# Cross-attention of a decoder kernel: the row maximum is subtracted by GpSimd in SBUF, the scores are turned by transposes, and the first layer is spread over all heads

## What is computed

```python
out_mem = _mlp(*upd, k_flat).reshape(x_in.shape)        # silu(x @ w1.T + b1) @ w2.T + b2
g1 = jax.nn.sigmoid(out_swa @ lin1.T)
g2 = jax.nn.sigmoid(out_mem @ lin2.T)
out_merged = g1 * out_swa + g2 * out_mem
x = _layernorm(x + out_merged[:, NUM_PM:, :], axis=-1)
# _L0_xattn_ref
q, k, v = proj(query, wq, bq), proj(key, wk, bk), proj(value, wv, bv)
scores = jnp.einsum('bhqd,bhkd->bhqk', q, k) / np.sqrt(KEY_SIZE)
scores = jnp.where(mask[:, None, :, :], scores, -1000000000.0)
attn = jax.nn.softmax(scores, axis=-1)
x = jnp.einsum('bhqk,bhkd->bhqd', attn, v)
```

## Time and profile before

| | us |
|---|---|
| median of three runs | 1099.61 (1094.72 to 1112.12) |
| the profiled execution | 1108.69 |
| its span, first to last instruction | 1106.6 |
| PE busy | 789.4 (71%) |
| DVE busy | 529.8 (48%) |
| ACT busy | 394.6 (36%) |
| POOL busy | 132.5 (12%) |
| chain that ended last | PE 55%, DVE 20%, issue 9%, ACT 7%, DMA 6% |

### The profile page before, as it was taken

One profiled execution on the slowest core, in us unless ns is written; L12 is line 12 of the kernel. 1 busy time (PEld: TensorE's weight loads), 2 busy tenths in 40 slices (PEclk: granted clock), 3 DMA queues, 4 the chain that ended last, 5 costly groups with the idle time before them and its releaser, 6 DMA issues.

```text
span 1106.6 us, 14903 instructions
## 1 busy us (share of the span) xinstructions
PE 789.4 (71%) x4778; PEld 519.8 (47%) x4778; DVE 529.8 (48%) x1947; ACT 394.6 (36%) x924; POOL 132.5 (12%) x143
## 2 busy tenths in 40 slices
PE   5888687968444986968958829992665675684674
PEld 4445353534121653644735617782453462462462
DVE  4244253433233936936838321113456456446556
ACT  3514344351112542633623513330343243243343
POOL 9100000000101013013021040003200300300000
PEclk8797998999566997987977959996886786886887
DMA  7400000000116044072050011311100100100000
GB/s 217 142 10 10 1 19 0 19 0 0 53 37 87 1 60 84 3 79 62 15 64 13 1 45 35 102 37 44 39 10 0 48 9 0 47 9 0 10 0 10
DMA packets 49235, 39.36 MB, mean 36 GB/s; under 512 B 11234, under 2 KB 42658, under 8 KB 49188
## 3 DMA queue, kind: packets, MB, share of 16 engines
q1 hardware_dynamic: 47140, 34.62, 14.9%
q0 software_dynamic: 2048, 4.20, 1.3%
HBM read 27.20 MB, written 11.60 MB: 35 GB/s over the span
## 4 chain that ended last, share of the span: by engine, by line
PE 55%; DVE 20%; issue 9%; ACT 7%; DMA 6%; SPq 2%; POOL 1%; DVEq 1%; ACTq 0%; POOLq 0%
PE bank L1292 4%; DMA q_stack<-parts_dram 4%; PE bank L1213 4%; PE bank L1202 4%; DVE R L2064 2%; PE bank L1096 2%; PE bank L954 2%; PE bank L1016 2%; PE bank L1099 2%; PE bank L1109 2%; PE bank L1098 2%; PE bank L886 2%; PE bank L1068 2%; PE bank L1023 2%; PE bank L977 2%
## 5 line engine op out<-in xcount | busy, mean ns | idle before, releaser
L1813 DVE CUSTOM_DVE_ANT_0 bank<-bank,add_q 128x256 f32<-128x256 f32 x256 | 100.5, 457 | 51.2 <-PE bank L1068 39.3
L1507 ACT ACTIVATE pT<-bank 128x512 f32<-128x512 f32 x128 | 76.1, 597 | 76.7 <-PE bank L1099 74.4
L1068 PE MATMUL bank<-k_stack,q_stack 96*128 96x256 bf16 x256 | 52.5, 306 | 45.8 <-DMA q_stack<-parts_dram 39.4
L1232 PE MATMUL bank<-ident,X 128*128 128x128 f32 x48 | 14.2, 419 | 85.3 <-DVE X L1921 85.3
L1096 PE MATMUL bank<-q_stack,k_stack 96*128 96x256 bf16 x256 | 70.4, 275 | 1.2 <-DVE mx L1813 1.2
L1098 PE MATMUL bank<-add_k,ident_b 128*128 128x256 bf16 x256 | 70.6, 276 | 0.0
L1099 PE MATMUL bank<-neg_max,head_sel 96*128 96x256 bf16 x256 | 70.5, 276 | 0.0
L1292 PE MATMUL bank<-XT,kpad 128*128 128x256 f32 (+1 forms) x256 | 62.3, 373 | 0.0
L1068 PEld LDWEIGHTS bank<-k_stack,q_stack 96*128 96x128 bf16 x256 | 25.8, 107 | 71.1 <-DMA q_stack<-parts_dram 33.6
L2021 DVE TENSOR_TENSOR cT<-bank,decay 128x384 f32<-128x384 f32 x64 | 35.7, 558 | 47.1 <-ACT decay L1585 46.8
L1532 ACT ACTIVATE he<-bank 128x324 f32<-128x324 f32 x64 | 28.2, 440 | 69.5 <-PE bank L1202 64.0
(11 more groups left out here) (402 smaller groups left out, 1807.1 us busy)
## 6 DMA issues: line engine op xcount, KB each, us to landing
k_stack<-parts_dram SPq DMA_DIRECT2D x48, 64.0 KB
q_stack<-parts_dram SPq DMA_DIRECT2D x24, 128.0 KB, 11.8
expert_in<-no_rows SPq DMA_DIRECT2D x8, 324.0 KB, 4.0
rows<-expert_in SPq DMA_DIRECT2D x8, 324.0 KB
expert_out<-rows_y SPq DMA_DIRECT2D x8, 324.0 KB
moe_w<-in_L_ffn_w_dram SPq DMA_DIRECT2D x1, 2048.0 KB
parts_dram<-k_parts SPq DMA_DIRECT2D x4, 384.0 KB, 2.5
parts_dram<-q_parts SPq DMA_DIRECT2D x12, 128.0 KB, 1.7
```

The lines of the kernel that those rows point to most:

```text
L1068: last = pe.matmul(q_bank(n)[:, c * S:(c + 1) * S], q_stack[:, h // 2, b * S + c * P:b * S + (c + 1) * P], k_stack[:, h // 2, h % 2, b * S ...
L1507: act.activation(pT[:, g % 2, j], k_bank(n)[:].rearrange("p (c q) -> p c q", c=QC), ACT.Exp).then_inc(exp_ready.sem, 1)
L1813: last = dve.tensor_tensor_reduce(sc, sc, add_q[:, b * QC + c, :], 1.0, 2.0 * NEG, ALU.add, ALU.max, mx[:, c, h:h + 1])
```

## The change

The second set of scores, the transposes of the maxima, `negated`, `mask_k` and `add_k` go. A head is now: PE makes its scores with the query on the partitions (`scores`, three heads ahead); DVE adds the mask, writes the result to SBUF (`shifted`, four slots) and takes the row maximum; GpSimd subtracts the maximum in place, by two instructions of 128x256; PE turns the four 128x128 blocks by f32 transposes (`scores_T`) into one of two PSUM banks; ACT takes the exponential. The MLP's Silu becomes Tanh and a biased copy (`z_of`) on ACT and a multiplication on DVE, with the factor 0.5 taken later. `keys` and `head` now stand between the heads by `pe_at`, `act_at` and `dve_at`. `stack` is split: `stack_k(0)` stands ahead of `save_q(0)`, and in the loop both are issued when the last scores are made. The outputs are turned and divided in halves.

```diff
-        AHEAD = 14
...
+        LEAD = 3
+        SLIDE = 4
+        s_shifted = signal("s_shifted", XU)
...
-            return bank[4 + n % 4] if n < 12 else (bank[4], bank[5], bank[2])[n % 3]
+            return bank[4 + n % 3]
...
-        def k_bank(n):
-            return bank[6 + n % 2] if n < 20 else bank[4 + n % 4]
+        def sT_bank(n):
+            return (bank[7], bank[3])[n % 2]
...
+        pe_at = {3: 0, 5: 1, 7: 2, 9: 3, 11: 4, 13: 5, 15: 6, 18: 7, 23: 8, 25: 9}
+        act_at = {3: 0, 5: 1, 7: 2, 9: 3, 11: 4, 15: 6, 21: 7, 23: 8}
+        dve_at = {7: 0, 9: 1, 11: 2, 13: 3, 15: 4, 17: 5, 19: 6, 22: 7, 25: 8, 28: 9}
+        o_at = {21: 0, 23: 1}
...
             save_k(0)
+            stack_k(0)
             save_q(0)
-            stack(0)
+            stack_q(0)
...
-                    sp.wait_ge(*sT_ready.at(i))
-                    stack(i + 1)
+                    sp.wait_ge(*s_ready.at(i))
+                    stack_k(i + 1)
+                    stack_q(i + 1)
...
-                pool.tensor_scalar(add_q[:], mask_q[:], -1.0, -NEG, ALU.add, ALU.mult)
-                pool.tensor_scalar(add_k[:], mask_k[:], -1.0, -NEG, ALU.add, ALU.mult).then_inc(masks_ready.sem, 1)
+                pool.tensor_scalar(add_q[:], mask_q[:], -1.0, -NEG, ALU.add, ALU.mult).then_inc(masks_ready.sem, 1)
...
             def mix(i, following):
+                for n in range(XU):
+                    wait_apart(pool, passed, *s_read.at(i, n + 1))
+                    for c in range(QC):
+                        last = pool.tensor_scalar(shifted[:, n % SLIDE, c, :], shifted[:, n % SLIDE, c, :], mx[:, n % SLIDE, c:c + 1], None, ALU.subtract)
+                    last.then_inc(s_shifted.sem, 1)
+                    if following and n == 4:
+                        split_k(i + 1)
                 if following:
-                    split_k(i + 1)
-                    wait_apart(pool, passed, *sT_ready.at(i))
                     masks(i + 1)
...
-                def scores_q(n):
+                pe.wait_ge(*slots_ready.before(i))
...
-                        pe.wait_ge(*s_read.at(i, n - 3 if n < 14 else n - 2))
+                    if n >= 3:
+                        pe.wait_ge(*s_read.at(i, n - 2))
...
+                def scores_T(n):
+
+                    pe.wait_ge(*s_shifted.at(i, n + 1))
+                    if n >= 2:
+                        pe.wait_ge(*exp_ready.at(i, n - 1))
...
-                        pe.matmul(dst, k_stack[:, h // 2, h % 2, b * S + c * P:b * S + (c + 1) * P],
-                                  q_stack[:, h // 2, b * S:(b + 1) * S], start=True, stop=False)
-                        pe.matmul(dst, ident_b[:], add_k[:, b * QC + c, :], start=False, stop=False)
-                        last = pe.matmul(dst, head_sel[:, h % 8, :], neg_max[:, (n // 8) % 2, :], start=False, stop=True)
+                        for k in range(QC):
+                            last = pe.transpose(sT_bank(n)[:, k * S + c * P:k * S + (c + 1) * P], shifted[:, n % SLIDE, c, k * P:(k + 1) * P], ident[:])
                     last.then_inc(sT_ready.sem, 1)
 
...
-                        values((g - 1) // G, (g - 1) % G)
-                outputs_T(1)
+                for n in range(LEAD):
+                    scores(n)
+                for n in range(XU):
+                    if n + LEAD < XU:
+                        scores(n + LEAD)
+                    scores_T(n)
+                    if n >= 5 and n % 4 == 1:
+                        values((n // 4 - 1) // G, (n // 4 - 1) % G)
+                    if n in o_at:
+                        outputs_T(0, o_at[n])
+                    if following and n == 1:
+                        keys(i + 1)
+                    if following and n in pe_at:
+                        head(i + 1, pe_at[n])
+                values(NB - 1, G - 1)
+                for c in range(QC):
+                    outputs_T(1, c)
                 if following:
-                    pe.wait_ge(*exp_ready.at(i))
+                    pe.wait_ge(*s_read.at(i))
+                    pe.wait_ge(*pv_ready.at(i))
                     values_of(i + 1)
...
                     act.wait_ge(*zT_b.at(i, n + 1))
-                    act.activation(hT[:, n, 0:T], bank[1][:], ACT.Silu, bias=b1_new[:, n:n + 1]).then_inc(hT_b.sem, 1)
+                    if n == 0 and not is_first(i):
+                        act.wait_ge(*x_plus.before(i))
+                    if n >= 2:
+                        act.wait_ge(*hT_b.at(i, n - 1))
+                    act.activation(hT[:, n, 0:T], bank[1][:], ACT.Tanh, bias=b1_half[:, n:n + 1], scale=0.5)
+                    act.activation(z_of[n % 2], bank[1][:], ACT.Identity, bias=b1_new[:, n:n + 1]).then_inc(z_act.sem, 1)
...
-                if following:
-                    keys(i + 1)
-                    for n in range(5):
-                        head(i + 1, n)
...
+                    if following and n == 1:
+                        keys(i + 1)
+                    if following and n in act_at:
+                        head(i + 1, act_at[n])
...
+                if n < FC:
+                    dve.wait_ge(*z_act.at(i, n + 1))
+                    dve.scalar_tensor_tensor(hT[:, n, 0:T], hT[:, n, 0:T], 1.0, z_of[n % 2], ALU.add, ALU.mult).then_inc(hT_b.sem, 1)
...
-                def negated(m):
...
                     wait_apart(dve, passed, *s_ready.at(i, n + 1))
+                    if n >= SLIDE:
+                        wait_apart(dve, passed, *sT_ready.at(i, n - SLIDE + 1))
                     for c in range(QC):
-                        sc = q_bank(n)[:, c * S:(c + 1) * S]
-                        last = dve.tensor_tensor_reduce(sc, sc, add_q[:, b * QC + c, :], 1.0,
-                                                        2.0 * NEG, ALU.add, ALU.max, mx[:, c, h:h + 1])
+                        last = dve.tensor_tensor_reduce(shifted[:, n % SLIDE, c, :], q_bank(n)[:, c * S:(c + 1) * S], add_q[:, b * QC + c, :], 1.0,
+                                                        2.0 * NEG, ALU.add, ALU.max, mx[:, n % SLIDE, c:c + 1])
                     last.then_inc(s_read.sem, 1)
 
...
+                    if n - LEAD - 1 in o_at:
+                        outputs_of(0, o_at[n - LEAD - 1])
+                    if following and n in dve_at:
+                        head(i + 1, dve_at[n], head_chain)
+                for c in range(QC):
+                    outputs_of(1, c)
```

149 lines of the change are left out of this document (42 added, 107 removed).

## The result

The changed kernel takes **1159.81 us** (median of four, 1156.34 to 1172.37) against 1100.89 (1094.72 to 1112.12) for the one before, measured beside it: a ratio of 1.057, with a 95% interval of 1.053 to 1.061. The forecast was 1084, its range 1066 to 1116. It is slower, and by more than the range allowed.

The account below looks back on a forecast made before the run. No single engine was taken to bound the span, though over half the chain of waits is TensorE. Prologue -8, step 0 -3.2, step 1 +2.4, steps 2 and 3 -6.7: -15.5 us, giving 1084 against 1099.6; range 1066 to 1116.

Parts of the forecast that it names:

- GpSimd, the unknown: Price of GpSimd's new 128x256 f32 subtraction in each head: 0.45 us, bounds 0.40 to 0.74; 29 us per step, below TensorE.
- The rival that has GpSimd as the bound: Main part of each step: at 0.74 us an instruction GpSimd sets the time, 1115; chance 0.18, of which 0.10 beyond 2%.
- The scatters stand in front (a): Start of steps 1 to 3: GpSimd issues eight scatters first, so the first transposes start 11.8 us after `slot_i`.
- The chain behind the last transposes, 18.5: End of each step: from the last transposes to `slot_i` takes 18.5 us, as now.
- No wait for `q_stack` in steps 1 to 3: End of step: the stack's DMA, 20.7 us, is released earlier and no longer ends last.
- Prologue -8: Before the loop: `stack_k(0)` ahead of `save_q(0)` gains 10.5 us, less 4 x 0.6 given back; net -8.
- The second activation: Before the loop: one ACT activation more per projection chunk gives back 4 x 0.6 us of the gain.
- TensorE saves 7 us a step: Scores of 32 heads: a head costs TensorE 0.66 us instead of 0.88, saving 7.0 us in a step.
- the cold term: Start of the main part: TensorE has idled, so its first 8 us run at the low clock, costing 2.8 us.
- The last step, 62.3: Step 3, without projections: 11.8 + 32 + 18.5 = 62.3 us from `slot_i` to `slot_i`.
- The SBUF port: Rival in the steps: DVE instructions with two SBUF inputs hold GpSimd up, three steps lose 9 us, 1094; chance 0.06.
- TensorE at the low level throughout: Rival in the main part: transposes at 0.21 us each throughout, main part near 80 us, some 1220; chance 0.06.

Follow-up runs that it names:

- micro: Kernel before plus 14 GpSimd instructions of several forms, issued while GpSimd has nothing else to do, to price each alone; 1094.2 us (one run).
- spread: split with GpSimd's eight scatters of a step issued one behind every fourth head of the next step; 1105.4 us, ratio 1.003 to 1.012 to before.
- late_k: Changed kernel with the prologue's order as before, queries' parts saved ahead of the keys' stacking; 1172.0 us, ratio 1.061 to 1.071 to before.
- early_k: Kernel before with one edit alone: in the prologue the keys' stacking is issued ahead of saving the queries' parts; 1082.1 us, ratio 0.981 to 0.995.
- best: spread with GpSimd's half of the subtraction as a two-input operation, the maximum spread by access pattern; 1089.9 us, ratio 0.989 to 0.997 to before.
- split: Changed kernel with half of each head's subtraction on VectorE, one head behind, half on GpSimd; 1107.7 us, ratio 1.004 to 1.012 to before.
- micro_port: Kernel before plus twelve two-input GpSimd subtractions released together with twelve VectorE instructions in the first stage; 1103.1 us, 1099.4 before beside it (one run each).

## Why the prediction was wrong

**The step that failed is "GpSimd, the unknown".** It took 0.45 us for the 128x256 subtraction, in bounds of 0.40 to 0.74; it is 0.92. The bounds came from rows chosen by count of inputs: a `TENSOR_SCALAR` that reads bytes and a `CAST`, and a `TENSOR_TENSOR`. Neither has this operation with an f32 input. The grouping by line and shape of the kernel before has one row that does:

```profile
L842 POOL TENSOR_SCALAR v_aug<-ctx_tok 128x512 f32<-128x512 f32 x4 | 6.0, 1493 | 227.6 <-DVE X L1921 227.6
```

Operation and both types are those of the new instruction; its operand is a constant, which micro puts 0.07 us below a value per partition. It takes 1.49 us for 512 elements, more than the two-input row beside it (1.16). Halved, it is 0.75, just above the whole range that I gave; with the 0.27 us that micro's rows for 256 and 128 columns leave as fixed cost, 0.88. I had left it out for its short rows of output. A lower bound of 0.75 would have turned the forecast: by my own sum 0.74 already gave 1115, and 2% slower began at 0.80.

**With the right price the working gives the result.** The rival that has GpSimd as the bound put the main part at 32 heads, 4.3 and 3. At 0.92 us that is 32 x 1.84 + 7.3 = 66.2 (measured 65.4), a middle step 11.8 + 66.2 + 18.5 = 96.5 (96.6 and 95.7), step 0 2.6 + 66.2 + 18.5 = 87.3 (88.2) and the last, without `split_k`, 11.8 + 58.9 + 18.5 = 89.2 (87.8). That is 77.3 us above the 292.2 that the forecast had for the four steps: 1084 + 77 = 1161, measured 1160. The steps come out within 1.5 us each. That the total comes so close is in part luck, for two errors cancel: the prologue gave 2.8 us more than forecast, and step 2 before was taken at 78.8 where the same code took 76.3 to 76.9 in other executions. The mechanism was named, and its chance (0.18) was set by a price with the wrong rows under it.

*Point by point:*

- *The scatters stand in front (a):* right. GpSimd is free at 424.56, 11.0 us behind `slot_i`; the first transposes come one head of GpSimd's later. But its worth was less than its length, as spread shows.
- *The chain behind the last transposes, 18.5:* right, 18.3 in step 1.
- *No wait for `q_stack` in steps 1 to 3:* right; the only one is the prologue's 9.79.
- *Prologue -8:* right in cause (late_k, early_k), short in size: -10.8. The order gives 12.5. The second activation may take 1.7 back (48.3 against early_k's 46.6; 2.4 forecast), but the start of one and the same prologue differs by 2.7 between executions, so this part isn't shown.
- *TensorE saves 7 us a step:* true of the work (57.7 to 51.6 us at full clock in step 1), not of the time. At the high clock the transposes do start 0.11 us apart; but the steps with more pauses had more low clock. best, in which GpSimd has slack, is the forecast's own case. Its main part took 58.4 us where 49.4 were forecast: TensorE busy 50.1 (forecast 40.3 + 2.8), idle 8.3 (6.3). The nine missing microseconds have three parts. The clock took 6.7 us and not 2.8, since 13.4 us of the busy time lie at the low level, and the cold term counted only the start. The work at full clock is 43.4 us and not 40.3, in part because the sum went by distances between starts, and the busy time has the tail of the last matmul in front of each pause. The waits are 2.0 longer.
- *The last step, 62.3:* 57.0 in best, where the scatters are spread: 2.9 us to the first transposes instead of 11.8, 36.1 for the main part instead of 32, 18.0 behind it. split, which has them in front, took 66.5.
- *The SBUF port:* I saw no sign and gave it 0.06. It exists (micro_port), and in the changed kernel it is small: the mean of the subtraction is 939 ns for a median of 922, some 4 us over 256. In best GpSimd's mean is 690 for 615 and VectorE's 399 for 350.
- *TensorE at the low level throughout:* no, but the granted clock of a step went from 0.90 to 0.80. Between the two cases that I had, none and all, lay the real one.

Why TensorE's middle step is no shorter than before even in best is settled as far as the low clock and the waits above. What sets the clock in a step, and whether a longer lead than three heads, more slots for `shifted` or another order of the pieces would do better, isn't shown: no run varies them. Nor is the Silu as Tanh and multiplication priced by itself.

## What to carry to other kernels

Price an unseen instruction by the row with the same operation and the same types, before any row with the same number of inputs or elements; where that row looks odd, it belongs in the bounds and not out of them. On GpSimd try the subtraction of a value per partition as a two-input operation with the value spread by the access pattern: one line gave 38 us here. And when a change is several edits, ask which of them stands alone: issuing twelve loads earlier in the prologue was worth more than all the rest, and needed none of it. Last, a microsecond of matmuls saved is not a microsecond gained: look at how much of TensorE's busy time lies at the low clock before and after.
